# A decoder layer on one Trainium2 core: lower gate half, cross bias and x widening on GpSimd, three hidden transposes on TensorE, new engine orders

## The reference

```
x = x + attn(layernorm(x))      # 16 query heads in 4 groups, rope, causal softmax, output projection
x = x + xattn(layernorm(x))     # one head, scores against ctx / 16, masked softmax, weighted sum of ctx
x = x + ffn(layernorm(x))       # width 704, int8-like quantise-dequantise of x, h and all weights

def ffn(x):
    xq, w1q, w2q = _ste(x), _ste(w_gate_up), _ste(w_down)   # q = round(v / scale), scale = max|v| / 127 per row
    gate, up = split(xq @ w1q.T)
    hq = _ste(silu(gate) * up)
    return hq @ w2q.T
```

## Time and profile before

| | us |
|---|---|
| median of 3 runs | 94.25 (93.41 to 94.74) |
| the profiled execution's own time | 95.33 |
| its span, first to last instruction | 92.4 |
| outside the span | 2.93 |
| busy: PE / DVE / POOL / ACT | 80.0 / 75.1 / 65.7 / 62.0 |

### The profile page before, as it was taken

How to read it: one execution, slowest core, us unless ns; L and a number is a source line. 1 busy time by engine, 2 the same in 40 slices (tenths; PEclk the granted TensorE clock), 3 DMA queues, 4 the chain that set the end, 5 groups by cost and what they waited for, 6 DMA issues and landing times.

```text
span 92.4 us, 2203 instructions
## 1 busy us (share of the span) xinstructions
PE 80.0 (87%) x699; PEld 60.8 (66%) x699; DVE 75.1 (81%) x206; ACT 62.0 (67%) x167; POOL 65.7 (71%) x125
## 2 busy tenths in 40 slices
PE   5999799979989899989999999778599897989740
PEld 3798479857857678748676778467368884765420
DVE  6057966499998889999999779879997999999450
ACT  0510244858798798897968696767977878668810
POOL 5358848932557898995728784877069799999970
PEclk9999999999999999999999999999999999999999
DMA  1999999996560478010001010101404042372134
GB/s 27 298 354 400 417 404 402 397 361 127 105 134 3 90 284 197 7 28 0 0 0 28 7 28 0 28 0 32 82 10 85 0 85 42 70 178 80 63 138 141
DMA packets 15842, 11.87 MB, mean 128 GB/s; under 512 B 11402, under 2 KB 14424, under 8 KB 15704
## 3 DMA queue, kind: packets, MB, share of 16 engines
q1 hardware_dynamic: 15594, 11.51, 41.2%
q10 hardware_dynamic: 238, 0.23, 1.0%
HBM read 8.00 MB, written 1.06 MB: 98 GB/s over the span
## 4 chain that ended last, share of the span: by engine, by line
DVE 22%; PE 20%; POOL 18%; DMA 14%; issue 10%; ACT 9%; SPq 4%; POOLq 0%; ACTq 0%; DVEq 0%
DMA w_raw<-in_w 14%; POOL gate_up L1227 7%; PE ps_s L506 6%; DVE y_rsum L930 4%; POOL y_out L1267 3%; POOL ffn L1259 3%; ACT gates L788 3%; DVE w_amax L980 2%; PE ps_y L448 2%; DVE qk_rot L925 2%; PE ps_q L400 2%; DVE rot L918 2%; ACT p_cross L694 2%; DVE w_amax L1010 2%; PE ps_s L436 2%
## 5 line engine op out<-in xcount | busy, mean ns | idle before, releaser
L1227 POOL TENSOR_TENSOR gate_up<-gates,out_rows 128x704 f32<-128x704 f32 x7 | 11.9, 1707 | 4.7 <-ACT gates L788 3.5
L355 PE MATMUL ps_r<-warm 128*128 128x256 bf16 x54 | 8.2, 310 | 1.1 <-DVE warm L842 1.1
L930 DVE RECIPROCAL y_rsum<-ps_y 128x128 f32<-128x128 f32 x8 | 7.6, 952 | 1.0 <-PE ps_y L451 0.9
L1197 POOL TENSOR_SCALAR_AFFINE_SELECT p_self_T<-p_self_T 128x512 f32<-128x512 f32 x8 | 5.1, 640 | 4.5 <-ACT p_self_T L678 4.5
L596 PE MATMUL ps_y<-w_T,h_T 128*128 128x256 bf16 (+1 forms) x42 | 6.5, 275 | 1.8 <-ACT ffn L776 1.7
L506 PE MATMUL ps_s<-gate_hi,x_int_T 128*128 128x352 f32 x28 | 7.5, 349 | 0.6 <-ACT gates L788 0.5
L506 PE MATMUL ps_s<-up_int,x_int_T 128*128 128x352 f32 x32 | 6.9, 338 | 0.8 <-DVE hid L1070 0.8
L355 PEld LDWEIGHTS ps_r<-warm 128*128 128x128 bf16 x54 | 5.9, 112 | 2.6 <-DVE warm L842 1.1
L506 PE MATMUL ps_s<-gate_lo,x_int_T 128*128 128x352 f32 x28 | 6.8, 322 | 0.0
L1192 POOL TENSOR_TENSOR rot_c<-rot,b_rope 128x128 f32<-128x128 f32 x8 | 4.2, 526 | 3.5 <-DVE rot L918 3.3
L596 PEld LDWEIGHTS ps_y<-w_T,h_T 128*128 128x128 bf16 (+1 forms) x42 | 3.5, 97 | 4.8 <-ACT ffn L776 2.5
(11 more groups left out here) (186 smaller groups left out, 264.8 us busy)
## 6 DMA issues: line engine op xcount, KB each, us to landing
ctxT<-in_ctxT SPq DMA_DIRECT2D x1, 1024.0 KB, 8.7
w_raw<-in_w SPq DMA_DIRECT2D x2, 512.0 KB, 11.9
ctx_aug<-in_ctx SPq DMA_DIRECT2D x1, 1024.0 KB, 17.0
out_x<-y_out SPq DMA_DIRECT2D x8, 128.0 KB, 1.7
x_aug<-in_x SPq DMA_DIRECT2D x1, 768.0 KB, 7.0
xT<-in_xT SPq DMA_DIRECT2D x1, 768.0 KB, 9.9
w_raw<-in_w SPq DMA_DIRECT2D x1, 704.0 KB, 14.7
out_rows<-scale_rows_dram SPq DMA_DIRECT2D x1, 480.0 KB, 4.7
```

What stands on the lines that cost most here:

```text
L355: nc.tensor.matmul(ps_r[:, 0:2 * T], warm[:, 0:P], warm[:, :], start=True, stop=True)
L930: nc.vector.reciprocal(y_rsum[j % 3][:, :], ps_ys).then_inc(s["y_rsum_done"], 1)
L1197: nc.gpsimd.affine_select(out=p_self_T[j % 3][:, :, :], in_=p_self_T[j % 3][:, :, :], compare_op=ALU.is_ge, fill=0.0, base=0, pattern=[[0, ...
L1227: nc.gpsimd.tensor_tensor(gate_up[j % 2][:, :, :], gate[j % 2][:, :, :], up_row.rearrange("p (i f) -> p i f", i=2), ALU.mult).then_inc(s[" ...
```

## The change

- `lower_gate(0)` and `lower_gate(1)` are computed on GpSimd instead of VectorE.
- `bias_cross(j)`, a 128x1 multiply for each batch, goes from VectorE to GpSimd.
- x_int of batches 0 to 5, transposed by DMA as before, is widened on GpSimd (`widen_x`, new semaphore x_int_T_wide) instead of on ScalarE; TensorE waits for either semaphore by `x_int_T_done`.
- `step_x` takes over `invert_x` and works on groups: batches 0 to 3 at once, then 4 and 5, then 6, then 7. Batches 0 to 2 thus get their step only after x2 of batch 3.
- `scale_rope` and the buffers rope_r are gone: `rotate` is now a scalar_tensor_tensor that takes r1 as its scalar and the rope table itself.
- `BY_DMA = 3`: only h 0 to 2 is widened on VectorE and transposed by DMA; h 3 to 6 is transposed on TensorE and copied out by ScalarE.
- The order lines of PE, ACT, DVE and POOL are written anew.

```diff
-    BY_DMA = 6
+    BY_DMA = 3
...
-            transpose_h(3)
-            transpose_h(4)
             store_out(0)
-            transpose_h(5)
...
+            def x_int_T_done(j):
+
+                if j < X_BY_DMA:
+                    done(pe, "x_int_T_wide", j)
+                else:
+                    done(pe, "x_int_T_ready", j - X_BY_DMA)
...
             def rotate(j):
 
-                free(dve, "rot_c_done", j, 3)
-                done(dve, "rope_r_ready", j)
+                if j == 0:
+                    dve.wait_ge(s["x_first_loaded"], 16)
+                free(dve, "qk_ready", j, 3)
+                done(dve, "r1_ready", j)
                 done(dve, "qkv_done", j)
-                nc.vector.tensor_tensor(rot[j % 3][:, :, :].rearrange("p (m t) n -> p m (t n)", m=2),
-                                        ps_q[:, 0:4 * QK].unsqueeze(1).to_broadcast([P, 2, 4 * QK]),
-                                        rope_r[j % 3][:, :, :].rearrange("p (m t) n -> p m (t n)", m=2), ALU.mult).then_inc(s["rot_done"], 1)
+                nc.vector.scalar_tensor_tensor(rot[j % 3][:, :, :].rearrange("p (m t) n -> p m (t n)", m=2),
+                                               ps_q[:, 0:4 * QK].unsqueeze(1).to_broadcast([P, 2, 4 * QK]), r1[:, j:j + 1],
+                                               rope_sb.rearrange("p (m t) n -> p m (t n)", m=2), ALU.mult, ALU.mult).then_inc(s["rot_done"], 1)
...
+            def step_x(first, n, count):
+
+                dve.wait_ge(s["x_amax_done"], n)
+                nc.vector.tensor_scalar(x_step[:, first:n], x_amax[:, first:n], 1.0 / QMAX, GUARD, ALU.mult, ALU.max).then_inc(s["x_step_done"], n - first)
+                dve.wait_ge(s["x_step_done"], n)
+                nc.vector.reciprocal(x_inv[:, first:n], x_step[:, first:n]).then_inc(s["x_inv_ready"], n - first)
...
-            def scale_rope(j):
...
+            def lower_gate(c):
+
+                done(pool, "gate_T_ready", c)
+                done(pool, "gate_hi_ready", c)
+                nc.gpsimd.tensor_tensor(gate_lo[:, c, :], gate_T[c], gate_hi[:, c, :].bitcast(F32), ALU.subtract).then_inc(s["gate_lo_ready"], 1)
+
+            def bias_cross(j):
+                done(pool, "c_scale_ready", j)
+                done(pool, "cross_negmax_done", j)
+                nc.gpsimd.tensor_scalar(c_bias[:, j:j + 1], c_negmax[:, j:j + 1], c_scale[:, j:j + 1], 1.0, ALU.mult, ALU.mult).then_inc(s["cross_bias_ready"], 1)
+
+            def widen_x(j):
+
+                pool.wait_ge(s[f"x_T_{j}_loaded"], 16)
+                nc.gpsimd.tensor_copy(x_int_T[:, j, :, :], x_T[:, j, :, :]).then_inc(s["x_int_T_wide"], 1)
...
-            drop_later_keys(5); rotate_c(7); rotate_sum(7); rstd_2(4); drop_later_keys(6); centre_ctx(7)
+            rotate_sum(6); rstd_2(3); bias_cross(3); lower_gate(0); drop_later_keys(5); lower_gate(1)
+            rotate_c(7); rotate_sum(7); rstd_2(4); drop_later_keys(6); bias_cross(4); whole_x2(2)
+            scale_x(0, 4, 1); rstd_2(5); widen_x(0); bias_cross(5); drop_later_keys(7); whole_x2(3); widen_x(1)
```

More of the change, by code:

```diff
@@ L115, in decoder_layer @@
         r1 = sb("r1", [P, B])
-        rope_r = [sb(f"rope_r{i}", [P, 4, 2 * QK]) for i in range(3)]
         rot = [sb(f"rot{i}", [P, 4, 2 * QK]) for i in range(3)]
@@ new lines, in _ @@
+            exp_self(6); square_2(3); evacuate_qk(7); quantise_x(0); exp_cross(4); square_1(5)
+            evacuate_cross_p(4); evacuate_q_max(7); quantise_x(1); evacuate_x1(5); exp_self(7); quantise_x(2)
+            square_1(6); exp_cross(5); tanh_gate(0); evacuate_cross_p(5); quantise_x(3); square_2(4)
+            evacuate_x1(6); tanh_gate(1); square_2(5); exp_cross(6); quantise_x(4); evacuate_cross_p(6)
+            quantise_x(5); evacuate_x1(7); square_1(7); quantise_h(0); exp_cross(7); silu_gate(2); quantise_h(1)
@@ new lines, in _ @@
+            evacuate_cross_p(7); square_2(6); silu_gate(3); quantise_x(6); scale_down_rows(0); square_2(7)
+            silu_gate(4); quantise_h(2); evacuate_x_int(6); quantise_x(7); silu_gate(5); scale_down_rows(1)
+            quantise_h(3); evacuate_x_int(7); silu_gate(6); evacuate_h(3); quantise_h(4); last_silu(0)
+            scale_down_rows(2); quantise_h(5); evacuate_h(4); last_silu(1); scale_down_rows(3); evacuate_h(5)
+            quantise_h(6); scale_down_rows(4); evacuate_h(6); scale_down_rows(5); last_quantise_h(0)
@@ L1274, in _ @@
-            rstd_2(1); scale_rope(6); centre_ctx(1); scale_rope(7); whole_x2(0); centre_ctx(2)
-            drop_later_keys(3); rotate_c(5); rotate_sum(5); centre_ctx(3); rstd_2(2); whole_x2(1); centre_ctx(4)
-            centre_ctx(5); drop_later_keys(4); rotate_c(6); rotate_sum(6); centre_ctx(6); rstd_2(3)
-            drop_later_keys(5); rotate_c(7); rotate_sum(7); rstd_2(4); drop_later_keys(6); centre_ctx(7)
-            whole_x2(2); rstd_2(5); scale_x(0, 4, 1); drop_later_keys(7); whole_x2(3); whole_x2(4); rstd_2(6)
@@ L1279, in _ @@
[L1279 to L1283 removed]
+            rstd_1(0, 1, 1); sum_bias(); rope_bias(); rotate_c(0); rotate_sum(0); rstd_1(1, 2, 2); rotate_c(1)
@@ new lines, in _ @@
+            rotate_sum(1); rstd_1(2, B, 3); drop_later_keys(0); rotate_c(2); rotate_sum(2); drop_later_keys(1)
+            centre_ctx(0); rotate_c(3); rotate_sum(3); centre_ctx(1); rstd_2(0); drop_later_keys(2)
+            bias_cross(0); centre_ctx(2); rotate_c(4); rotate_sum(4); centre_ctx(3); centre_ctx(4); rstd_2(1)
+            centre_ctx(5); bias_cross(1); drop_later_keys(3); rotate_c(5); rotate_sum(5); centre_ctx(6)
+            whole_x2(0); rstd_2(2); centre_ctx(7); bias_cross(2); drop_later_keys(4); whole_x2(1); rotate_c(6)
@@ new lines, in _ @@
+            rotate_sum(6); rstd_2(3); bias_cross(3); lower_gate(0); drop_later_keys(5); lower_gate(1)
+            rotate_c(7); rotate_sum(7); rstd_2(4); drop_later_keys(6); bias_cross(4); whole_x2(2)
+            scale_x(0, 4, 1); rstd_2(5); widen_x(0); bias_cross(5); drop_later_keys(7); whole_x2(3); widen_x(1)
+            whole_x2(4); rstd_2(6); widen_gate(0); bias_cross(6); widen_x(2); whole_x2(5); widen_x(3)
+            widen_gate(1); rstd_2(7); bias_cross(7); widen_x(4); widen_x(5); scale_x(4, 6, 2); widen_gate(2)
```

179 lines of the change are left out of this document (69 added, 110 removed).

## The result

The changed kernel takes 97.78 us (median of 4, 97.50 to 98.01), the one before 94.38 (median of 4, 93.41 to 94.74). The ratio is 1.038, with a 95% interval of 1.029 to 1.046: slower, and above the predicted range. The profiled execution takes 97.8 us, its span is 95.9 (92.4 before). So 3.5 us are lost inside the span, while 1.9 us instead of 2.93 lie around it. All ratios here compare the runs that lie within 1.5% of their kernel's fastest one.

The account below looks back on a forecast made before the run. DVE and PE were taken as both near their limit, with POOL holding the slack. Terms of +0.1, 0 and +0.5 gave +0.6 us on the 94.25 median, 94.9 us (own range 93.3 to 96.0; 91.9 to 97.0 overall).

Parts of the forecast that it names:

- Step 1: Up to bias_cross(3): with less queued on DVE, its result comes at 41.8 us instead of 43.5, a gain of 1.7.
- rival 1: POOL is late: scale_gate(1) and lower_gate(0) collide, rotate_c(7) starts at 48.7, time 97.1 us; chance 0.15 full, 0.07 in part.
- Step 2: From bias_cross(3) to the first gate product: POOL's queue takes 11.1 us, product at 52.9 against 52.75, +0.1.
- Step 3: First feed-forward batches: silu_gate(2) stays where it is, 0 with ends of -1.5 and +1.5 us.
- Step 4: The end, silu_gate(6) to the last quantisation on ACT: 10.3 us against 9.80 before, +0.5.
- three signs: Wrong if the first gate matmul is before 51.9 us, gate_lo on POOL nearer 0.9, or ACT unwaiting at the end.
- Rival 2: Relief of DVE wins: bias 2.7 us earlier, first gate product at 51.9, end costs nothing, time 92.0 us; chance 0.25.
- Rival 3: Widening x on POOL takes 0.8 us instead of 0.48, about 1 us is passed on, time 95.9 us; chance 0.05.

Follow-up runs that it names:

- lower_dve: The changed kernel with the two lower_gate put back on VectorE; ratio 1.047 (1.041 to 1.053) to the kernel before.
- bias_dve: The changed kernel with the eight bias_cross put back on VectorE; ratio 1.030 (1.022 to 1.037) to the kernel before.
- orders_only: The changed kernel's new orders with the moved work back on its old engines, scalar rotation kept; ratio 1.037 (1.029 to 1.045) to the kernel before.
- b_h3: The kernel before with only h of batches 3 to 5 transposed by TensorE and copied out by ScalarE; ratio 1.033 (1.027 to 1.039).
- b_pool_two: The kernel before, own orders, with scalar rotation and both lower_gate and the eight bias_cross on GpSimd; ratio 1.063 (1.057 to 1.069).
- pick2: The kernel before with scalar rotation, bias_cross(7) on GpSimd, and scale_x(4, 6, 2), finish_gate(1), gate_product(2), quantise_h(0) re-ordered; ratio 0.988, median 93.76 us.

## Why the prediction was wrong

**Step 1 failed.** It took 1.7 us as gained at T0, 41.8; the bias of batch 3 was there at 44.3, 0.8 us later than in the kernel before. These 2.5 us are most of the miss of 2.9. Four things are in them. This execution started late: lower_dve, with an early start, begins the same bias at 42.78, not 43.35, 0.6 us. The bias instruction took 0.94 us instead of 0.26, while scale_gate(1) ran on DVE, 0.7. Biases on POOL hold up exp_cross, and it PE, as at 40.22: bias_dve, also with an early start, has the bias at 42.29, 1.4 us before lower_dve, of which 0.7 are the instruction, so 0.7 are left for this. The last 0.5 us stay open. The step named PE's 1.9 idle us as the limit of the gain, and was silent on the price of the moved wait: it took eight biases off DVE's queue as a gain and charged them to POOL as 0.192 us each. The right question was who waits for each. Its collision of DVE and POOL, held back for rival 1, came true already here, with the bias in place of lower_gate.

**Step 2 had its queue right, and not what the queue decides.** 11.1 us from T0 to the product were predicted, 11.1 measured, with the POOL cast as releaser. But PE reached the product only at 54.46, so a faster POOL could have given 0.9 us. The step also read the earlier trace rows wrongly where it began: the product at 52.75 has no wait in its row and was not released by exp_self(7); it follows project_out(6), 52.40, in PE's queue. And the transfer of x 0 is hardly covered: quantise_x(0) came at 50.06, not 48.1, and by the estimate above it landed at 53.7 to 54.0, with the cast at 54.86. Rival 1 gives almost the measured number (97.1, rotate_c(7) at 48.7, measured 48.14) and is still not the cause: in lower_dve, with rotate_c(7) at 45.86, well under its threshold of 46.6, the time was no better.

**Step 3** predicted no loss behind the product; silu_gate(2) is 0.2 us nearer to it than before, so the term is right, by two errors that cancel. exp_cross(7) is 4.3 us late (66.43, before 62.12) and the table load came at 67.02, not 64.6; but quantise_h(0), which stood between that exp and the load, stands ahead of the exp now. orders_only, whose product comes 1.25 us earlier, has its silu_gate(2) even later (68.85 against 68.32). The walk through the order checked each wait against the state at hand, and took the order for a neutral carrier of the edits.

**Step 4.** 10.55 us against 10.3 predicted and 9.80 before. Right: ACT waits 0.51 and 0.49 us at the casts of batches 5 and 6, where 0.3 to 0.5 were named; at that of batch 4 it doesn't wait. b_h3 shows that it depends on the new orders.

Of the three signs by which the prediction would have called itself wrong, none came: the product was not early, gate_lo took 1.68 us and ACT does wait at the end. They guarded against a gain in the wrong place, not against T0 late.

**What was never priced** is the new orders by themselves. They cost 3.5 us without any move (orders_only); the moves cost 5.9 and 3.1 under the old orders (b_pool_two, b_h3), and no loss beyond the orders' own is seen under the new ones. So the orders hide the waits of the moves, and cost 3.5 us themselves. Rival 2 fell: DVE was busy 29.60 us between 7.5 and 43.3 (30.70 before), and its marks came later. Rival 3 fell: the widening takes 0.40.

Left open: why the first half of the new orders costs 2%, beyond the waits shown, and how much of it is in the changed kernel. No kernel here undoes the grouped steps of x or the widening on POOL alone, so their price is not known; the late quantise_x(0) is theirs.

## What to carry to other kernels

A short instruction between two engines is priced by who waits for it, not by its length: eight of 0.2 us each, moved to a queue with longer ones, cost 4.6 us. Which engine is right for it depends on its place in the queue: pick2 has the bias of batch 7 on POOL, right behind rstd_2(7) where POOL was idle, and ACT waits 0.48 us for it, 0.74 when it was on DVE. Price a change of order as a part of its own, by building the new order without the moves. And a late mark with a busy engine ahead of it is not yet a cause: the two big instructions that stood there cost 0.4% of the time and 1.2 us of the span.
